# Two more places for experts in the first stage of an adapter + mixture-of-experts layer, their requests ahead of x and of W's last pieces, and the first residual in quarters

## The reference

```python
Bx = einsum('bni,bri->bnr', x, cond_B[ids])          # rank 16
y = einsum('bnr,bor->bno', Bx, cond_A[ids])
base_out = einsum('bsi,oi->bso', y, base_w) + base_b
res_hidden = einsum('bsi,ri->bsr', y, ffn_A)
probs = softmax(einsum('bsi,ei->bse', y, router_w))
topw, topi = top_k(probs, 2)
topw = topw / (sum(topw) + 1e-06)
combine = sum(one_hot(topi, 16) * topw[..., None], axis=-2)
delta = einsum('bse,bsr,eor->bso', combine, res_hidden, ffn_B)
return x + base_out + delta * 0.5
```

## Time and profile before

| | us |
|---|---|
| runs | 462.93, 463.29, 459.8 |
| median | 462.93 |
| profiled execution | 459.67 |
| its span | 457.4 |
| TensorE busy / VectorE busy / ScalarE busy | 413.4 / 312.7 / 107.5 |
| mean granted TensorE clock | 0.991 |

### The profile page before, as it was taken

The page is one execution under the profiler, slowest core; times in us unless marked ns, Lnnn a source line. Parts: engine busy times, 40 slices in busy tenths (PEclk is TensorE's granted clock), DMA queues, the critical chain, the costliest instruction groups (busy, mean ns, idle before and its releaser), DMA issues.

```text
span 457.4 us, 6130 instructions
## 1 busy us (share of the span) xinstructions
PE 413.4 (90%) x2240; PEld 275.5 (60%) x2240; DVE 312.7 (68%) x702; ACT 107.5 (24%) x163; POOL 40.5 (9%) x53
## 2 busy tenths in 40 slices
PE   0687996799888999999999999999999999999996
PEld 0466884576555675566567556655675566566675
DVE  3699699698457557766767675677667766757353
ACT  0002033345563240132013102400230132123210
POOL 3020000002100120012001101200120012002000
PEclk9998999899999999999999999999999999999999
DMA  8999999899999998898989998988998899555835
GB/s 230 362 335 334 336 377 346 267 234 322 333 320 235 346 348 267 282 347 301 296 287 367 306 289 294 367 269 292 331 334 282 289 361 309 194 195 196 322 148 185
DMA packets 90383, 135.30 MB, mean 296 GB/s; under 512 B 5506, under 2 KB 43442, under 8 KB 90354
## 3 DMA queue, kind: packets, MB, share of 16 engines
q1 hardware_dynamic: 63680, 102.08, 67.2%
q10 hardware_dynamic: 26674, 32.84, 23.9%
HBM read 99.23 MB, written 35.65 MB: 295 GB/s over the span
## 4 chain that ended last, share of the span: by engine, by line
PE 68%; DVE 13%; DMA 12%; issue 2%; ACT 2%; ACTq 2%; DVEq 0%
PE ps L871 13%; PE ps L892 12%; PE ps L893 10%; PE ps L894 10%; DMA early_u<-in_L_ffn_B 7%; PE ps L905 7%; PE ps L895 5%; DMA xbuf<-in_L_ffn_base_w 5%; PE ps L826 3%; DVE xT L706 3%; DVE h_r L687 3%; PE ps L836 3%; DVE early L639 3%; ACT bexpT L473 2%; DVE xbuf L814 2%
## 5 line engine op out<-in xcount | busy, mean ns | idle before, releaser
L814 DVE TENSOR_TENSOR xbuf<-ps,xbuf 128x512 f32<-128x512 f32 x128 | 86.9, 679 | 110.4 <-PE ps L895 110.2
L892 PE MATMUL ps<-h_r,u_r 128*128 128x512 f32 x256 | 109.4, 427 | 7.1 <-DVE xbuf L814 7.1
L893 PE MATMUL ps<-h_r,u_r 128*128 128x512 f32 x256 | 100.3, 392 | 0.0
L894 PE MATMUL ps<-h_r,u_r 128*128 128x512 f32 x256 | 100.1, 391 | 0.0
L836 PE MATMUL ps<-early 128*128 128x256 f32 x256 | 65.7, 409 | 20.3 <-DVE early L639 20.2
L892 PEld LDWEIGHTS ps<-h_r,u_r 128*128 128x128 f32 x256 | 48.0, 188 | 47.6 <-issue 20.1
L706 DVE STREAM_TRANSPOSE xT<-xbuf 128x512 f32<-128x512 f32 x112 | 72.0, 681 | 0.0
L836 PEld LDWEIGHTS ps<-early 128*128 128x128 f32 x256 | 49.5, 204 | 32.9 <-issue 17.6
L639 DVE STREAM_TRANSPOSE early<-xbuf 128x256 f32<-128x256 f32 x128 | 66.1, 581 | 4.3 <-issue 3.7
L871 PE MATMUL ps<-bexpT,cur 128*32 128x512 f32 x512 | 61.6, 598 | 2.2 <-DVE h_r L687 1.5
L473 ACT ACTIVATE h_r<-ps 128x512 fp32r<-128x512 f32 x64 | 35.7, 594 | 87.6 <-issue 54.9
(11 more groups left out here) (67 smaller groups left out, 207.1 us busy)
## 6 DMA issues: line engine op xcount, KB each, us to landing
out<-xbuf SPq DMA_DIRECT2D x31, 1024.0 KB, 7.0
xbuf<-in_x SPq DMA_DIRECT2D x28, 1024.0 KB, 7.0
xbuf<-in_x SPq DMA_DIRECT2D x32, 512.0 KB, 8.4
xbuf<-in_x ACTq DMA_DIRECT2D x32, 512.0 KB, 9.5
xbuf<-in_L_ffn_base_w SPq DMA_DIRECT2D x16, 512.0 KB, 18.6
xbuf<-in_L_ffn_base_w ACTq DMA_DIRECT2D x16, 512.0 KB, 19.1
gm_r<-g_hilo SPq DMA_DIRECT2D x128, 32.0 KB, 6.5
early_u<-in_L_ffn_B SPq DMA_DIRECT2D x12, 256.0 KB, 15.5
```

Of the source, the lines that this page charges most:

```text
L814: dve.tensor_tensor(xs, ps[:, ACC + t % 2, :], xs, ALU.add).then_inc(s_out, 1)
L892: pe.matmul(acc, u_r[:, b.q, 0, h, tok_t], hi, start=(h == 0), stop=False)
L893: pe.matmul(acc, u_r[:, b.q, 0, h, tok_t], lo, start=False, stop=False)
L894: pe.matmul(acc, u_r[:, b.q, 1, h, tok_t], hi, start=False, stop=False)
```

## The change

Groups 0 to 9 use places 0 to 4 instead of 0 to 2: group 3 takes place 4, group 4 place 3 (for which it waits on the bias rows), groups 5 to 9 then follow on places 0, 1, 2, 0, 1. Groups 10 and 11 take places 3 and 4 again. Group 4 is requested ahead of x on both queues, group 5 ahead of W's piece 6, 6 ahead of piece 7, and 7 right behind it. VectorE's transposes of x's blocks 4 and 6 wait, for batch 0 as for batch 1, until the group in the place has been flipped.

The first residual comes in quarters of two token tiles by two column quarters; quarters 0 and 2 need transpose 80, 1 and 3 transpose 96, and each is requested earlier in the order. The additions of batch 0 wait for the quarter of their tokens and columns.

```diff
-        E_SLOT = (0, 1, 2, 0, 1, 2, 0, 1, 2, 0, 3, 4, 5, 6, 0, 1)
-        E_LOAD_AT = {31: 3, 50: 4, 62: 5, 75: 6, 83: 7, 89: 8, 93: 9, 102: 10, 103: 11, 106: 12, 110: 13, 117: 14, 120: 15}
+        E_SLOT = (0, 1, 2, 4, 3, 0, 1, 2, 0, 1, 3, 4, 5, 6, 0, 1)
+        E_LOAD_AT = {31: 3, 32: 4, 51: 5, 63: 6, 64: 7, 89: 8, 93: 9, 102: 10, 103: 11, 106: 12, 110: 13, 117: 14, 120: 15}
         PIECE_AT, X0_AT = {26: 5, 51: 6, 63: 7}, 32
         GLO_AT = 40
-        XRES_AT, XQ_AT = {97: 0, 112: 1, 119: 2}, 108
+        XRES_AT, XQ_AT = {81: 0, 97: 1, 112: 2, 119: 3}, 108
...
             if e_users(g):
                 eng.wait_ge(s_ef, e_users(g)[-1] + 1)
+            if g == 4:
+                eng.wait_ge(s_biasrow, 32)
             elif g in (10, 11):
...
-        def load_first_xres(eng, c, h):
-
+        def load_first_xres(eng, k, h):
+
+            eng.wait_ge(s_wt, (5 + k % 2) * KD)
             half = slice(h * (P // 2), (h + 1) * (P // 2))
-            eng.dma_start(xres[half, :, c * BANK:(c + 1) * BANK],
-                          x_v[0, half, :, c * BANK:(c + 1) * BANK]).then_inc(s_xres[c], 16)
+            ts, cols = slice(k % 2 * 2, k % 2 * 2 + 2), slice(k // 2 * 2 * BANK, (k // 2 + 1) * 2 * BANK)
+            eng.dma_start(xres[half, ts, cols], x_v[0, half, ts, cols]).then_inc(s_xres[k], 16)
...
             load_experts(sp, 3, 0)
+            load_experts(sp, 4, 0)
             load_x0(sp, (0, 1))
             store_g(0)
-            load_experts(sp, 4, 0)
+            load_experts(sp, 5, 0)
             load_w(sp, 6, (0, 1))
-            load_experts(sp, 5, 0)
+            load_experts(sp, 6, 0)
             load_w(sp, 7, (0, 1))
+            load_experts(sp, 7, 0)
             store_g(1)
-            for g in range(6, 9):
-                load_experts(sp, g, 0)
+            load_first_xres(sp, 0, 0)
+            load_experts(sp, 8, 0)
             load_experts(sp, 9, 0)
-            sp.wait_ge(s_wt, 6 * KD)
-            load_first_xres(sp, 0, 0)
+            load_first_xres(sp, 1, 0)
             load_gm(0, 0)
...
             load_experts(sp, 13, 0)
-            load_first_xres(sp, 1, 0)
+            load_first_xres(sp, 2, 0)
             load_gm(0, 1)
             load_experts(sp, 14, 0)
-            load_first_xres(sp, 2, 0)
+            load_first_xres(sp, 3, 0)
             load_experts(sp, 15, 0)
             sp.wait_ge(s_wt, 8 * KD)
             load_xquad(sp, 1, 1, (0, 1))
             store_g(3)
-            load_first_xres(sp, 3, 0)
...
                 if n in XRES_AT:
-                    act.wait_ge(s_wt, 6 * KD)
                     load_first_xres(act, XRES_AT[n], 1)
...
             load_xquad(act, 1, 1, (2, 3))
-            load_first_xres(act, 3, 1)
...
-                if f.n == 1 and j in (4, 6):
-                    dve.wait_ge(s_ef, E_SLOT.index(j // 2 + 1) + 1)
+                if f.n < 2 and j in (4, 6):
+                    dve.wait_ge(s_ef, [g for g in range(GROUPS) if E_SLOT[g] == j // 2 + 1][f.n] + 1)
...
-                        if t == 0:
+                        if b.n == 0 and m % 2 == 0:
+                            dve.wait_ge(s_xres[c // 2 * 2 + t // 2], 32)
+                        elif t == 0:
                             dve.wait_ge(s_xres[c], b.n * 16 + 32)
```

## The result

The changed kernel takes 457.73 us (median of 19 runs) against 460.71 for the one before on the same chips (19 runs): ratio 0.9926, 95% interval 0.9906 to 0.9945. That is 3.4 us of 460.71, between 2.5 and 4.3, and is within 1%. The two medians differ by 3.0. The profiled execution took 457.73 with a span of 455.9; against the profiled one before (459.67) it gained 1.9 us, of which 1.5 lie in the span. It shows less than the medians because the execution profiled before was 1.0 us faster than its median, and this one is just its median.

A forecast was written before the change was run, and what follows sets the result against it. It took the first stage as bound by expert groups awaiting places, then the full DMA, stalling TensorE and VectorE. Stalls of 3.59 and 0.49 go, x costs 0.4, logits pass 4.0 us earlier: 462.93 - 4.0 = 458.9 us, range 455.4 to 462.0.

The forecast's parts named there:

- The sum: First stage up to the logits: VectorE's stalls of 3.59 and 0.49 us go, x costs 0.4; 4.0 us earlier.
- rival 1: First stage: x in time, group 7 by 88, no wait for logits; gain 4.9 us, 458.0 us; chance 0.20.
- What is late next: Before flips 7: group 7 lands at 88.5 to 89.2, TensorE wants it at 86.7, about 2 us late.
- flips 0.9, three products 1.3, x products 1.98: TensorE's work after group 7 lands: 4.2 us, so the second x products end at about 92.9.
- the clock's fall for the gap before flips 4: TensorE idles some 3 us there; if its clock falls, VectorE loses 0.7 us; left out of the sum.
- x: x's first transposes: with group 4 ahead, x lands at 71.0 and VectorE waits 0.4 us, bounds 0 and 2.
- ScalarE's issues: Near 70 us: one more issue takes 2.5 us, copy of group 3 starts at 72.5, flips 4 end at 75.8; hidden.
- Rival 4: ScalarE stands at its full queue, 9.03 us an issue, delaying expert copies: 7 us slower, 470; chance 0.05.
- Rival 3: ScalarE's issues cost 5 us each: gain 1.4 us, 461.5, or 0 if the clock also falls, 462.9; chance 0.13.
- Without it the gain would stand: Early first quarter of the residual: the gain doesn't need it, as the first addition came at 121.
- It fills the dry stretch: Requesting the residual's first quarter at transpose 80, not 96, uses DMA bandwidth left free behind 85 us.
- a sign of being right: DMA from 85 to 100 us: 340 GB/s or more would show the prediction right.

The follow-up runs named there:

- e1: Changed kernel with the first residual as in the kernel before, so only the experts' places and requests: 458.31 us against 461.07, ratio 0.9947.
- e2: Kernel before with only the residual in quarters and its earlier requests: 462.62 us against 461.07, ratio 1.0040.
- e6: Changed kernel with group 7 requested last, behind g and the first quarter of the residual: 463.53 us against 461.66 for the kernel before, ratio 1.0034.
- e8: Changed kernel with ScalarE's issue of group 7 moved behind its copy of group 3: ratio 0.9933 to the kernel before.
- e7: Changed kernel with group 4 requested behind x, not ahead of it: ratio 0.9932 to the kernel before.
- e5: Changed kernel with group 7 ahead of W's piece 7 and ScalarE's issues of groups 10 and 11 behind its copy of the x products' sum: 456.23 us, ratio 0.9900.
- e12: Changed kernel, group 7 ahead of piece 7, groups 10 and 11 behind the copy, residual quarters behind transpose 96 and groups 8 and 9: 456.00 us, ratio 0.9896.
- e3: Changed kernel with group 7 requested ahead of W's piece 7 on both queues: 457.06 us, ratio 0.9925 to the kernel before.
- e10: The changed kernel itself, unaltered, measured again beside others on one chip: 458.52 us, ratio 0.9945 to the kernel before.

## Why the prediction was right, step by step

- **The sum.** 4.0 us were forecast and 3.4 (2.5 to 4.3) measured, 3.0 by the difference of the two medians. The mechanism is in the main the one named: the places gate the requests, and groups that land late hold up TensorE. e1 has the gain without the residual, and the profile has the 3.59 us gone. In one point the prediction misread its rows: only group 5 gates product 90 and with it x's block 8. Group 6's flips (88.86) come after block 8 (84.97); what they hold up is the second x products and the logits, and by e2 that is the chain that sets the time.
- **Luck in the number.** The forecast of 458.9 was 462.93 - 4.0, and the median of the kernel before came down to 460.71 over 19 runs: on that level the same sum gives 456.7, and 457.73 was measured. A level 2.2 us too high and a gain 1.0 too large offset each other in part; 457.73 lies below the forecast's own range (458.3 to 459.9) and next to rival 1's 458.0, whose conditions (group 7 in by 88, no wait for the logits) didn't come. And the 4.0 us at the logits stand in no profile of the changed kernel: 1.35 in the first, 0.6 in the second (99.94), 2.9 in e1's. Of the kernel before there is only one profile, so it isn't known how its median execution differs.
- **What is late next.** Group 7 was named, with 88.5 to 89.2 us and a wait of TensorE of about 2 us. It landed at 89.5, and TensorE was there a microsecond earlier than taken, at 85.8, as group 6 was in time and the flips before it ended at 82.6: the wait is 3.71. e6 shows that a later one costs in full (4.7 us later, 4.1 to 5.0 us slower).
- **The term that was mis-sized is what follows that wait.** The step "flips 0.9, three products 1.3, x products 1.98" priced it at the full clock. In the profile the clock fell (0.66 from 90 to 95 us) with the gap of 3.71 us before it: from the start of the flips (89.49) to the x products (93.47) passed 3.98 us where the step has 2.2, 1.8 more, and x's products ended at 95.4 and not 92.9. The prediction weighed the clock's fall for the gap before flips 4, at 0.7 us, and not for this one, which it took for 2 us; its rows had no fall behind 2.41. The Trainium skill ("TensorE: Matmul & The Clock Gate", "HAM oscillation — how this bites in real kernels") describes this pattern, a wait for DMA behind which the next matmuls run at half the clock; the trace agrees for the 3.71 us, and has the 1.61 us of e1 without it. In e1's profile the same wait is 1.6 us, the clock stays, and the logits come at 97.62. The length of the gap alone doesn't decide here: the clock fell behind 2.75 us (e8) and 3.13 (e7), and not behind 3.24 (e1).
- **x.** 0.4 us were charged. The profile has none: 70.36 without a wait. Other profiles have 0.3 (e5), 1.2 (e1) and 1.9 us (e8, where VectorE came early), inside the bound of 2. With group 4 behind x (e7) nothing was gained.
- **ScalarE's issues.** Copy 3 was dated 72.5 and came at 70.91; flips 4 ended at 74.3 (75.8 forecast), in time for block 4 at 75.71, and e8 shows that the stand costs nothing that can be measured. Rival 4 is out: no two issues of ScalarE between 57 and 100 us took more than 5.12 together. Rival 3's half, the clock's fall behind the gap before flips 4, didn't come in the changed kernel's profile but does occur: e7's has it, with stalls of 0.83 and 2.22 us against the 0.7 priced.
- **The residual.** "Without it the gain would stand" held (e1). "It fills the dry stretch" did not, and neither did its price of nothing where it stands alone: 1.8 us (e2); in the changed kernel itself no price of it was told from noise. The stretch of 85 to 100, where 340 GB/s was named as a sign of being right, has 338 GB/s to 90 and then 244 at a full busy share.
- **Behind the stage.** The period of 42.4 us and the shift by one number were right (1.35 us at the logits, 1.4 at 165.99 and 208.42).
- **Outside the span** no gain was forecast. The profiled execution has 1.8 us there and not 2.3, and every run of e1 to e12 has 1.8 to 2.0, where the kernel before has 2.1 to 2.3 on every chip it was measured on again. So some 0.4 us of the gain are none of the mechanism's. It is there also in e2, without the places. Why, no run tells.

## What to carry to other kernels

Where a queue is full, date each transfer by the bytes ahead of it and compare with when its reader arrives: this told which group would be late next. Putting that one ahead of a piece with 10 us of cover had no gain alone (e3), and 1.2 to 1.8 us together with a shorter chain behind it, within overlapping intervals. With the residual left as it was besides, the ratio is 0.9878, 5.6 us under the kernel before and clear of the changed one. Ask also which of two waits the end depends on: the largest stall of VectorE was not it (e2). Price a wait of TensorE also with the clock that may come after it, and as a chance: the gap of 3.71 us cost 1.8 us more than itself and the one of 1.61 nothing, but 2.75 us had a fall behind it in one profile and 3.24 had none in another. And a transfer that nobody waits for isn't free to move early: it is in the way of the next one that somebody does.

## What was not expected of the hardware

**The first stage loses clock at different places from execution to execution.** The kernels have a gap of TensorE of 2.0 to 3.0 us that ends near 43 us. In both first profiles the clock falls right behind it and is back by 50 us. That isn't free: VectorE waits for TensorE's 32 matmuls there, in the changed kernel 3.83 us, and in e8, whose clock is 1.00 all through to 85 us, 2.38:

```profile
48.84 0.60 DVE L657 TENSOR_SCALAR table<-ps 64x128 f32<-64x128 f32 x2 [3.83 <-PE ps L854]
```

```profile
47.53 0.60 DVE L657 TENSOR_SCALAR table<-ps 64x128 f32<-64x128 f32 x2 [2.38 <-PE ps L854]
```

But e8's lead is lost again at x, whose data it has to wait for (1.91 us, at 71.04; the changed kernel is at x at 70.36 without a wait). In other executions the clock falls some microseconds later, and once more at 55 to 60 us, and then VectorE is late at x. The changed kernel in its second measurement:

```profile
40.00:45.00 5.00, 2.36 (x11) 1.67 (x10) 4.96 (x9) 0.00 (x0) 0.00 (x0) 0.93 1.06 352
45.00:50.00 5.00, 5.00 (x33) 4.95 (x32) 0.92 (x3) 0.00 (x0) 0.00 (x0) 0.73 1.07 332
...
55.00:60.00 5.00, 5.00 (x18) 4.36 (x18) 3.06 (x8) 1.42 (x2) 0.22 (x1) 0.50 1.07 345
```

```profile
59.43 0.62 DVE L640 STREAM_TRANSPOSE early<-xbuf 128x256 f32<-128x256 f32 x1 [1.73 <-PE ps L839]
...
99.94 0.23 DVE L729 TENSOR_REDUCE mx<-ps 128x4 f32<-128x64 f32 x1 [0.79 <-PE ps L916]
```

and the first one in the stretch where it differs:

```profile
55.00:60.00 5.00, 5.00 (x28) 4.49 (x27) 5.00 (x11) 2.22 (x2) 0.22 (x1) 1.00 1.07 351
```

With a clock of 0.50 from 55 to 60, VectorE, eight buffers ahead, waits 1.73 us and then three times up to 0.24 for a product, and stands at x's first block at 74.4 in place of 70.4. After that there is no wait before flips 7 at all, TensorE comes when the group is there, and the logits come at 99.94. So a late TensorE hides a late group, and the two losses don't add. This may be why putting group 7 first gained nothing in e3, but only its slowest run was profiled, and that has the 0.50. It is likely one source of the spread between runs of one kernel: in e10 the fastest run (455.76) had a mean clock of 0.995 and the slowest (461.18) 0.985. What decides where the clock falls was not found.

**A DMA at full share and low rate.** In the changed kernel 95 to 100 us have a share of 1.06 and 201 GB/s; 60 to 80 us had the same share at 361. The stretch holds the second quarter of the residual, experts and the reads of g. Which of them is slow, and for what, was not measured, so a full share alone doesn't tell how much is moved.
